# Sending routed rows with a rolling wait of three on four semaphores, in place of groups of four

## The chip, the cores and the metric

The kernel runs on one core of one Trainium2 chip. The metric is the device time of one execution, in microseconds (us); lower is better. The kernel before takes 642.34 us, the median of 3 runs (642.05 to 642.77).

## The reference

Four sequences of 1024 tokens with 256 channels pass through an attention-like block and then a mixture of experts. What matters here is the second part: every token picks two of eight experts, and its normalised row takes part in both.

```python
x = x + _layernorm(_L0_attn_ref(_layernorm(x), Wq, Wk, fc1_w, fc1_b, fc2_w, fc2_b))
x = x + _layernorm(_L0_ffn_ref(_layernorm(x), gate_w, gate_b, w1, b1, w2, b2))

# attention: rotated q and k in bf16, exp(scores) summed over the causal keys,
# one number per token, then 1 -> 16 -> 256 with a relu between
# experts:
logits = flat @ gate_w + gate_b            # 4096 tokens, 8 experts
topv, topi = lax.top_k(logits, 2)
topw = softmax(topv)
for each expert e:
    h = gelu(flat @ w1[e] + b1[e])         # 256 -> 1024
    out = h @ w2[e] + b2[e]                # 1024 -> 256
    final += out * routing[:, e]
```

## The kernel before

The work has two stages that overlap a little.

**First stage, four sequences one after another ("batches" 0 to 3).** TensorE projects, scores and turns; ScalarE takes the exponentials; VectorE measures, normalises, chooses the two experts of each token and computes for each of its two copies a row number in `sorted_x`, a table in HBM where every expert has a region. `place_rows` (VectorE) ends with the semaphore `rows_ready`. GpSimd (POOL) then sends the batch: 16 indirect DMAs (8 tiles of 128 tokens, two copies), each of 128 rows of 260 numbers (`send_rows`, line 185). A row holds the token's 256 normalised channels and 4 numbers (the "tag": token, first expert, two weights). Batches 0 to 2 are sent from `xrows`, batch 3 from `xrow_last`.

**Second stage, tiles of 256 sorted rows.** SyncE (SP) loads a tile `xt` from `sorted_x` (line 527 for tiles 0 and 1, line 1474 from tile 2 on). TensorE turns it (`pX`, line 455), multiplies by `w1` (`pL`, line 1623, 48 matmuls) and by `w2` (`pY`, line 1635, 48 matmuls), each as three products of high and low halves. VectorE splits the hidden values (`h_lo`, line 1652), and GpSimd adds the two halves of the result `y` to their tokens in `sum_y` with two indirect DMAs (line 533), called scatters below. Tiles 0 and 1 belong to the busiest expert and are computed while batch 3 is still in the first stage; from tile 2 on the loops of `over_tiles` run.

**What sets the order around the change.** Every engine executes its own instructions in order. Those of GpSimd are, for batches 0 to 2: wait for `rows_ready`, four sends, wait until the whole group has landed, four sends, and so on; after the last group `rows_left` is raised. For batch 3 the sends stand without such waits between the scatters of tiles 0 and 1: sends 0 to 5, scatters of tile 0, sends 6 and 7, wait for tile 0's scatters, scatters of tile 1, sends 8 to 10, wait for tile 1's scatters (`y_left`), sends 11 to 15. Then comes the block of tiles 2 and on: it waits for the steering table, reads the number of tiles of the expert (line 1413), and for each tile waits for `y_ready`, issues two scatters, waits until they have landed (`y_sent`) and raises `y_left` (line 77).

VectorE needs `y_left` before it computes the weights of the next tile (`weigh_rows`, line 1661); behind that stand in its order the copy of the tag (`save_tag`, line 464), the taking of `y` (line 1671) and the splitting of the next tile's hidden values. SP loads the next `xt` only once the tag has been copied.

SP itself waited for `rows_sent` to reach the count of two whole batches before it loaded tile 0, and for three or four whole batches from tile 2 on (`load_tile`).

Of the kernel before, what the change touches and what calls it, by code (L numbers as in the profile page):

```python
# [21 lines left out]
B, L, D = 4, 1024, 256  # L22
NT = B * L
KC = D // P
TB = L // P
# [9 lines left out]
AHEAD = 2  # L35
# [22 lines left out]
BATCH_SENT = 2 * TB * 16  # L58
SP_ENDS = 4
END_SENT = NE * 16  # L60
SEND_FIRST = (6, 8, 11)
BURST = 4


RSQRT_LINKS = 10
# [8 lines left out]
def hold(eng, sem, value, passed):  # L74

    eng.wait_ge(sem, value)
    eng.sem_inc(passed, 1)
# [39 lines left out]
def build(nc, x_in, wqT, wkT, fc1_w, fc1_b, fc2_wT, fc2_b, low_rows, gate_w, gate_b, w1, b1T, w2, b2,  # L117
# [7 lines left out]
    with ExitStack() as ctx:  # L125
        def sb(name, shape, dt, c=ctx):
            return c.enter_context(nc.sbuf_tensor(name, shape, dt))

        def sem(name, c=ctx):
            return c.enter_context(nc.semaphore(name))  # L130
# [29 lines left out]
        sb("rows_kept", [P, TB, XW], F32)  # L160
        fill = sb("fill", [P, TM // P, XW], F32)
        slot_i = sb("slot_i", [P, 2 * 2 * TB], I32)
        rows_sent = sem("rows_sent")
        tile_in = sem("tile_in")
        b1_taken = sem("b1_taken")
        passed = sem("passed")
# [7 lines left out]
        def load_second(sp, e, par):  # L174
# [2 lines left out]
                         w2[bass.ds(e, 1), :, :].rearrange("e (c p) d -> p (e c) d", p=P)  # L177
                         ).then_inc(weights_in[par][1], 16)

        def send_rows(pool, c, which):  # L180

            rows = xrow_last if c == B - 1 else xrows[:, c * TB:(c + 1) * TB, :]
            for i in which:
                at = c % 2 * 2 * TB + i
                pool.indirect_dma_start(  # L185
                    out=sorted_x, out_offset=bass.IndirectOffsetOnAxis(ap=slot_i[:, at:at + 1], axis=0),
                    in_=rows[:, i % TB, :], in_offset=None).then_inc(rows_sent, 16)

# [217 lines left out]
        rows_left = sem("rows_left")  # L408
# [70 lines left out]
        def _(sp):  # L479
# [39 lines left out]
            e1 = sp.value_load(busy_i[0:1, 2:3].bitcast(I32), min_val=0, max_val=NE - 1)  # L519
            load_first(sp, e1, 1)  # L520
            load_second(sp, e1, 1)
            sp.wait_ge(rows_sent, AHEAD * BATCH_SENT)
            for g in range(AHEAD):
                if g > 0:
                    sp.wait_ge(tile_turned, g)
# [6 lines left out]
        def scatter_rows(pool, i, rows, to, sent=y_sent):  # L532
            pool.indirect_dma_start(  # L533
                out=sum_y, out_offset=bass.IndirectOffsetOnAxis(ap=to[:, i:i + 1], axis=0),
                in_=rows[:, i, :], in_offset=None,
                compute_op=ALU.add).then_inc(sent, 16)

        @block.gpsimd
        def _(pool):
            def scatter_ahead(pool, g):  # L540

                for i in range(TM // P):
                    pool.wait_ge(y_ready, 2 * g + i + 1)
                    scatter_rows(pool, i, ys_ahead[g], dests_ahead[g])

            pool.sem_inc(rows_left, 2)
# [12 lines left out]

            for b in range(B - 1):  # L560
                pool.wait_ge(rows_ready, b + 1)
                for first in range(0, 2 * TB, BURST):
                    if first > 0:
                        hold(pool, rows_sent, b * BATCH_SENT + first * 16, passed)
                    send_rows(pool, b, range(first, first + BURST))
                hold(pool, rows_sent, (b + 1) * BATCH_SENT, rows_left)

            pool.sem_inc(y_left, ONE)
            pool.wait_ge(sums_cleared, 16)
# [6 lines left out]
            send_rows(pool, B - 1, range(SEND_FIRST[1], SEND_FIRST[2]))  # L576
            hold(pool, y_sent, 64, y_left)
            send_rows(pool, B - 1, range(SEND_FIRST[2], 2 * TB))

        @block.scalar  # L580
        def _(act):
# [882 lines left out]
        def _(sp):  # L1464
# [4 lines left out]

            def load_tile(sp, word):  # L1470

                hold(sp, rows_sent, (word & 1) * BATCH_SENT + (B - 1) * BATCH_SENT, passed)
                hold(sp, ends_filled, (word & 1) * END_SENT + ONE, passed)
                sp.dma_start(xt[:], sorted_x[bass.ds(word >> 1, TM), :].rearrange("(a p) c -> p a c", p=P)
                             ).then_inc(tile_in, 16)
# [17 lines left out]
            word = tile_word(sp, 0)  # L1493
# [4 lines left out]
            word = tile_word(sp, 1)  # L1498
# [3 lines left out]
            word = sp.value_load(steer[0:1, C_TILES + NP - 1:C_TILES + NP], min_val=0, max_val=WORD_MAX)  # L1502
# [339 lines left out]
```

## Time and profile before

| | before |
|---|---|
| median of 3 runs | 642.34 us |
| the profiled execution | 638.7 us |
| its span | 636.9 us |
| mean granted TensorE clock | 0.936 |
| TensorE matmul busy | 545.6 us, 86% |
| VectorE busy | 424.5 us, 67% |
| ScalarE busy | 365.3 us, 57% |
| GpSimd busy | 187.3 us, 29% |

The span is the profiled execution from its first to its last instruction; 1.8 us of its time lie outside. A busy share is an average over both stages. From about 234 us on the path is mostly TensorE's, save where the experts change; before that it shares the path with VectorE and others. For each send or scatter the profile shows GpSimd's time to write the descriptors, about 1 us for a send and 1.6 us for a scatter; the data moves after that, on queue q0 (SP's transfers move on q1).

### The profile page before, as it was taken

Reading aid. Unit: us, or ns where it says so; the run is one execution under the profiler, and the core shown is the slowest. Engines: PE = TensorE matmul, PEld = TensorE weight load, DVE = VectorE, ACT = ScalarE, POOL = GpSimd, SP = SyncE. Lnnn points to the kernel's source line nnn. Section 1 sums busy time; section 2 is a strip of 40 time slices with the busy share of each in tenths; the row PEclk is TensorE's granted clock in tenths of the full one; section 3 lists DMA queues with packets and bytes.
Section 4 is the critical chain, followed back from the end, with each engine's and each line's share of the span. In section 5 each row is a group of like instructions: output and inputs, shape, how many; then the busy total and the mean of one; then the engine's idle time right before and its main releaser. Section 6 shows DMA issues by size and latency. Waiting matters only on the chain.

```text
span 636.9 us, 14628 instructions
## 1 busy us (share of the span) xinstructions
PE 545.6 (86%) x4170; PEld 500.3 (79%) x4175; DVE 424.5 (67%) x1444; ACT 365.3 (57%) x836; POOL 187.3 (29%) x153
## 2 busy tenths in 40 slices
PE   1968788686896989999999999999999999999940
PEld 1737365462775989999999989989998999998940
DVE  5799698996887665545555557487388655455477
ACT  3455766684570746364554665685688563553582
POOL 2000045244535653242322412312312232421320
PEclk9968969798797999999999999999999999999985
DMA  8930011362215833232232353384374232322479
GB/s 216 361 118 1 1 67 67 114 236 87 90 43 185 237 87 60 50 44 39 52 48 50 45 161 63 58 247 91 46 246 88 51 50 50 44 39 50 99 186 326
DMA packets 51853, 66.79 MB, mean 105 GB/s; under 512 B 4870, under 2 KB 45292, under 8 KB 51692
## 3 DMA queue, kind: packets, MB, share of 16 engines
q1 hardware_dynamic: 37804, 47.87, 23.9%
q0 software_dynamic: 14016, 18.56, 16.9%
q8 instruction: 11, 0.18, 0.1%
q14 instruction: 22, 0.18, 0.1%
HBM read 38.26 MB, written 28.74 MB: 105 GB/s over the span
## 4 chain that ended last, share of the span: by engine, by line
PE 68%; DVE 16%; issue 5%; ACT 4%; DMA 4%; POOL 1%; DVEq 1%; SPq 0%; POOLq 0%; ACTq 0%
PE pY L1635 28%; PE pL L1623 24%; PE pP L759 6%; DMA sum_y<-y,dest 3%; PE pP L861 2%; PE pS L776 2%; PE pX L455 2%; DVE z L1775 2%; DVE mstats L1003 2%; PE pT L744 1%; ACT probs L657 1%; PE pS L818 1%; ACT xrows L631 1%; POOL sum_y L533 1%; DMA x_all<-x 1%
## 5 line engine op out<-in xcount | busy, mean ns | idle before, releaser
L1558 ACT ACTIVATE h<-pL,b_now 128x256 f32<-128x256 f32 x272 | 112.3, 463 | 151.7 <-PE pL L1623 146.7
L533 POOL DMA_INDIRECT sum_y<-y,dest x68 | 110.2, 1621 | 269.4 <-DVE y L1679 256.9
L1635 PE MATMUL pY<-w_hi,h_lo 128*128 128x256 f32 x544 | 154.0, 283 | 3.5 <-DVE h_lo L1652 3.4
L1623 PE MATMUL pL<-xeT_hi,w_lo 128*128 128x256 f32 x544 | 151.4, 278 | 6.2 <-issue 6.1
L1652 DVE TENSOR_TENSOR h_lo<-h,h_hi 128x512 fp32r<-128x512 f32 x136 | 92.7, 691 | 91.7 <-ACT h_hi L1564 90.9
L1635 PE MATMUL pY<-w_hi,h_hi 128*128 128x256 f32 x544 | 150.7, 277 | 0.6 <-issue 0.6
L1623 PE MATMUL pL<-xeT_lo,w_hi 128*128 128x256 f32 x544 | 150.7, 277 | 0.0
L1635 PE MATMUL pY<-w_lo,h_hi 128*128 128x256 f32 x544 | 150.6, 277 | 0.0
L1623 PE MATMUL pL<-xeT_hi,w_hi 128*128 128x256 f32 x544 | 150.6, 277 | 0.0
L1623 PEld LDWEIGHTS pL<-xeT_hi,w_lo 128*128 128x128 f32 x544 | 102.0, 188 | 7.6 <-issue 7.6
L1635 PEld LDWEIGHTS pY<-w_hi,h_lo 128*128 128x128 f32 x544 | 102.2, 188 | 5.1 <-DVE h_lo L1652 4.6
L1635 PEld LDWEIGHTS pY<-w_lo,h_hi 128*128 128x128 f32 x544 | 102.4, 188 | 0.8 <-issue 0.8
L1635 PEld LDWEIGHTS pY<-w_hi,h_hi 128*128 128x128 f32 x544 | 102.3, 188 | 0.0
L1623 PEld LDWEIGHTS pL<-xeT_lo,w_hi 128*128 128x128 f32 x544 | 102.1, 188 | 0.0
L1623 PEld LDWEIGHTS pL<-xeT_hi,w_hi 128*128 128x128 f32 x544 | 102.1, 188 | 0.0
L1564 ACT ACTIVATE h_hi<-h 128x512 fp32r<-128x512 f32 x136 | 86.0, 632 | 6.3
L185 POOL DMA_INDIRECT sorted_x<-xrows,slot_i x48 | 49.2, 1026 | 128.5 <-DVE xrows L1144 89.6
L1671 DVE SCALAR_TENSOR_TENSOR y<-pY,b_all 128x256 f32<-128x256 f32 x66 | 27.8, 421 | 44.5 <-PE pY L1635 44.5
L200 DVE TENSOR_TENSOR w_lo<-w_stage,w_hi 128x512 fp32r<-128x512 f32 x64 | 42.4, 688 | 14.4 <-ACT w_hi L193 9.1
L193 ACT ACTIVATE w_hi<-w_stage 128x512 fp32r<-128x512 f32 x64 | 36.8, 620 | 0.0
L744 PE MATMUL pT<-ident,xn 128*128 128x128 f32 x64 | 17.6, 430 | 19.2 <-ACT xn L588 11.3
L608 ACT ACTIVATE qk<-pP 128x512 bf16<-128x512 f32 x32 | 19.0, 592 | 21.5 <-PE pP L759 20.4
(292 smaller groups left out, 847.5 us busy)
## 6 DMA issues: line engine op xcount, KB each, us to landing
w_stage<-w SPq DMA_DIRECT2D x16, 1024.0 KB
xt<-sorted_x SPq DMA_DIRECT2D x38, 260.0 KB
sum_y<-fill SPq DMA_DIRECT2D x1, 4352.0 KB, 19.9
w_stage<-sum_y SPq DMA_DIRECT2D x8, 512.0 KB, 8.0
out<-z SPq DMA_DIRECT2D x8, 512.0 KB, 5.9
x_all<-x SPq DMA_DIRECT2D x3, 1024.0 KB, 8.3
sorted_x<-fill SPq DMA_DIRECT2D x8, 260.0 KB
sum_y<-y,dest POOLq DMA_INDIRECT x68, 3.7
```

Of the source, the lines that this page charges most:

```text
L185: pool.indirect_dma_start(out=sorted_x, out_offset=bass.IndirectOffsetOnAxis(ap=slot_i[:, at:at + 1], axis=0), in_=rows[:, i % TB, :], in_ ...
L193: act.activation(w_hi[par][:, i, q * WQ:(q + 1) * WQ], w_stage[par][:, i, q * WQ:(q + 1) * WQ], ACT.Copy).then_inc(w_hi_ready[i], 1)
L200: low = dve.tensor_tensor(w_lo[par][:, i, piece], w_stage[par][:, i, piece], w_hi[par][:, i, piece].bitcast(F32), ALU.subtract)
L533: pool.indirect_dma_start(out=sum_y, out_offset=bass.IndirectOffsetOnAxis(ap=to[:, i:i + 1], axis=0), in_=rows[:, i, :], in_offset=None, c ...
L744: mm = pe.transpose(pT[:, n % 2, u * P:(u + 1) * P], xn[:, t, k * P:(k + 1) * P], ident[:])
L759: mm = pe.matmul(pP[:, n % 2, :], w[:, k, i, mo], x[:, k, tok], start=(k == 0 and w is wqk_lo), stop=(k == KC - 1 and x is xT_lo))
L1558: a = act.activation(h[:, c, :], pL[:, bk, i * TM:(i + 1) * TM], ACT.Gelu, bias=b1_now[par][:, c:c + 1])
L1564: act.activation(h_hi[:, 2 * bk:2 * bk + 2, :], h[:, 2 * bk:2 * bk + 2, :], ACT.Copy).then_inc(h_hi_ready, 1)
L1623: mm = pe.matmul(pL[:, bk, i * TM:(i + 1) * TM], w[:, 0, col], x[:, k, :], start=(k == 0 and w is lo), stop=(k == KC - 1 and x is xeT_lo))
L1635: mm = pe.matmul(pY[:, i, 0:D], s[:, c, rows], w[:, 1, c * D:(c + 1) * D], start=(c == 0 and s is h_lo), stop=(c == FC - 1 and w is lo))
L1652: dve.tensor_tensor(h_lo[:, cs, :], h[:, cs, :], h_hi[:, cs, :].bitcast(F32), ALU.subtract).then_inc(h_split, 1)
L1671: dve.scalar_tensor_tensor(out=y[:, i, :], in0=pY[:, i, 0:D], scalar=1.0, in1=b2_all[:, bass.ds(who, 1), :].rearrange("p e d -> p (e d)"), ...
```

## The change

The sends go to four semaphores in turn, `rows_sent0` to `rows_sent3`. Send i of a batch, for i of 3 and more, first waits until send i-3 has landed. After the 16th the last three are waited for, and `rows_left` is raised; this is new for batch 3. The scatters of tiles 0 and 1 have such a wait too. SP waits for `rows_left` where it waited for `rows_sent`.

```diff
-BURST = 4
+LANES = 4
+LAG = 3
...
-        rows_sent = sem("rows_sent")
+        rows_sent = [sem(f"rows_sent{lane}") for lane in range(LANES)]
...
+        def landed(pool, c, i):
+
+            pool.wait_ge(rows_sent[i % LANES], c * BATCH_SENT // LANES + (i // LANES + 1) * 16)
+
         def send_rows(pool, c, which):
 
             rows = xrow_last if c == B - 1 else xrows[:, c * TB:(c + 1) * TB, :]
             for i in which:
                 at = c % 2 * 2 * TB + i
+                if i >= LAG:
+                    landed(pool, c, i - LAG)
                 pool.indirect_dma_start(
                     out=sorted_x, out_offset=bass.IndirectOffsetOnAxis(ap=slot_i[:, at:at + 1], axis=0),
-                    in_=rows[:, i % TB, :], in_offset=None).then_inc(rows_sent, 16)
+                    in_=rows[:, i % TB, :], in_offset=None).then_inc(rows_sent[i % LANES], 16)
...
-            sp.wait_ge(rows_sent, AHEAD * BATCH_SENT)
+            sp.wait_ge(rows_left, 2 + AHEAD)
...
                     pool.wait_ge(y_ready, 2 * g + i + 1)
+                    landed(pool, B - 1, SEND_FIRST[g] - LAG + i)
                     scatter_rows(pool, i, ys_ahead[g], dests_ahead[g])
...
                 pool.wait_ge(rows_ready, b + 1)
-                for first in range(0, 2 * TB, BURST):
-                    if first > 0:
-                        hold(pool, rows_sent, b * BATCH_SENT + first * 16, passed)
-                    send_rows(pool, b, range(first, first + BURST))
-                hold(pool, rows_sent, (b + 1) * BATCH_SENT, rows_left)
+                send_rows(pool, b, range(2 * TB))
+                for i in range(2 * TB - LAG, 2 * TB):
+                    landed(pool, b, i)
+                pool.sem_inc(rows_left, 1)
...
             send_rows(pool, B - 1, range(SEND_FIRST[2], 2 * TB))
+            for i in range(2 * TB - LAG, 2 * TB):
+                landed(pool, B - 1, i)
+            pool.sem_inc(rows_left, 1)
...
-                hold(sp, rows_sent, (word & 1) * BATCH_SENT + (B - 1) * BATCH_SENT, passed)
+                hold(sp, rows_left, (word & 1) + 2 + B - 1, passed)
```

GpSimd's instructions from a batch of the middle, before. One row is one instruction or several alike; in brackets stand the semaphores that it waits for.

```order
L185 DMA sorted_x<-xrows,slot_i 34816x260 [waits rows_sent,rows_ready]
L185 DMA sorted_x<-xrows,slot_i 34816x260 x3
L185 DMA sorted_x<-xrows,slot_i 34816x260 [waits rows_sent]
L185 DMA sorted_x<-xrows,slot_i 34816x260 x3
L185 DMA sorted_x<-xrows,slot_i 34816x260 [waits rows_sent]
```

The same place in the changed kernel, its first seven sends:

```order
L192 DMA sorted_x<-xrows,slot_i 34816x260 [waits rows_sent3,rows_sent1,rows_sent2,rows_ready]
L192 DMA sorted_x<-xrows,slot_i 34816x260 x2
L192 DMA sorted_x<-xrows,slot_i 34816x260 [waits rows_sent0]
L192 DMA sorted_x<-xrows,slot_i 34816x260 [waits rows_sent1]
L192 DMA sorted_x<-xrows,slot_i 34816x260 [waits rows_sent2]
L192 DMA sorted_x<-xrows,slot_i 34816x260 [waits rows_sent3]
```

No send has moved. One wait in four sends has become one at each from the fourth on.

GpSimd from the wait for tile 1's scatters to the first scatter of tile 2, before:

```order
L185 DMA sorted_x<-xrow_last,slot_i 34816x260 [waits y_sent]
L185 DMA sorted_x<-xrow_last,slot_i 34816x260 x4
L1527 UNCONDITIONAL_BRANCH
L1451 UNCONDITIONAL_BRANCH [waits steer_ready]
L1451 ISA
L1413 TENSOR_LOAD steer
L1413 ISA x2
L1438 REGISTER_ALU
L1438 COMPARE_AND_BRANCH
L76 REGISTER_ALU x2
L76 ISA
L533 DMA sum_y<-y,dest 4352x256 [waits y_ready]
```

The same place in the changed kernel:

```order
L192 DMA sorted_x<-xrow_last,slot_i 34816x260 [waits y_sent,rows_sent0]
L192 DMA sorted_x<-xrow_last,slot_i 34816x260 [waits rows_sent1]
L192 DMA sorted_x<-xrow_last,slot_i 34816x260 [waits rows_sent2]
L192 DMA sorted_x<-xrow_last,slot_i 34816x260 [waits rows_sent3]
L192 DMA sorted_x<-xrow_last,slot_i 34816x260 [waits rows_sent0]
L1537 UNCONDITIONAL_BRANCH [waits rows_sent3,rows_sent1,rows_sent2]
L1461 UNCONDITIONAL_BRANCH [waits steer_ready]
L1461 ISA
L1423 TENSOR_LOAD steer
L1423 ISA x2
L1448 REGISTER_ALU
L1448 COMPARE_AND_BRANCH
```

The branch that leaves the first stage now waits for the last three sends; all that follows on GpSimd stands behind it.

## Rows read from the trace of the kernel before

**Rows 1.** The page's busy time: engine, us (share of the span) x instructions.

```profile
PE 545.6 (86%) x4170; PEld 500.3 (79%) x4175; DVE 424.5 (67%) x1444; ACT 365.3 (57%) x836; POOL 187.3 (29%) x153
```

**Rows 2.** The chain that ended last, 240 to 637: start us, us, what.

```profile
251.75 0.44 PE pX L455 x4
252.19 5.46 PE pY L1635 x48
```

**Rows 3.** The chain again, 196 to 245.

```profile
213.07 8.30 DMA sum_y<-y,dest
...
221.39 0.03 POOLq L77
...
224.25 2.23 DMA xt<-sorted_x
...
234.97 5.44 PE pL L1623 x48
240.41 0.44 PE pX L455 x4
```

**Rows 4.** Timeline of GpSimd, 78 to 125: start, us, instruction [idle before, releaser].

```profile
82.27 1.06 POOL L185 DMA_INDIRECT sorted_x<-xrows,slot_i  x1 [76.68 <-DVE xrows L1144]
...
86.22 0.97 POOL L185 DMA_INDIRECT sorted_x<-xrows,slot_i  x1 [0.30 <-issue]
89.48 0.96 POOL L185 DMA_INDIRECT sorted_x<-xrows,slot_i  x1 [2.29 <-DMA sorted_x<-xrows,slot_i]
```

**Rows 5.** Line 77, whole span: count, ns min/median/max, first and last start.

```profile
L77 POOLq EVENT_SEMAPHORE  x114: 17/17/17, 88.7 to 614.1; - x114
```

**Rows 6.** Timeline of GpSimd, 125 to 245: inside batch 1, and the start of batch 3.

```profile
130.34 0.96 POOL L185 DMA_INDIRECT sorted_x<-xrows,slot_i  x1 [6.49 <-DMA sorted_x<-xrows,slot_i]
...
193.98 0.97 POOL L185 DMA_INDIRECT sorted_x<-xrow_last,slot_i  x1 [10.66 <-DVE xrow_last L1144]
```

**Rows 7.** Timeline of SP, 100 to 275: loads of tiles 0 and 1.

```profile
153.48 4.42 SPq L527 DMA_DIRECT2D xt<-sorted_x  x2
```

**Rows 8.** Timeline of VectorE, 146 to 176: the tag of tile 0.

```profile
156.26 0.20 DVE L464 COPY tag<-xt 128x8 f32<-128x8 f32 x1
```

**Rows 9.** Timeline of TensorE, 150 to 170.

```profile
156.24 1.11 PE L804 MATMUL pT<-ident,xt 128*128 128x128 f32 x4 [3.86 <-DMA xt<-sorted_x]
158.61 1.12 PE L787 MATMUL pT<-ident,hid 128*128 128x128 f32 x4 [1.26 <-DVE hid L994]
```

**Rows 10.** Window 160 to 166: length, engines' busy us, then PEclk, DMA share, GB/s.

```profile
160.00:166.00 6.00, 5.58 (x28) 5.36 (x29) 4.47 (x23) 3.30 (x7) 3.04 (x4) 0.50 0.23 83
```

**Rows 11.** Timeline of GpSimd, 125 to 245, from batch 3's send 11 on.

```profile
222.17 0.96 POOL L185 DMA_INDIRECT sorted_x<-xrow_last,slot_i  x1 [3.23 <-DMA sum_y<-y,dest]
...
227.50 1.50 POOL L185 DMA_INDIRECT sorted_x<-xrow_last,slot_i  x1 [0.30 <-issue]
229.30 1.61 POOL L533 DMA_INDIRECT sum_y<-y,dest  x1 [0.30 <-issue]
231.21 1.91 POOL L533 DMA_INDIRECT sum_y<-y,dest  x1 [0.30 <-issue]
```

**Rows 12.** GpSimd's queue in 229 to 230, then 230 to 231: packets, MB, share.

```profile
q0 software_dynamic: 40, 0.12, 33.3%
...
q0 software_dynamic: 8, 0.01, 4.3%
```

**Rows 13.** GpSimd's sequencer: line 1451 in 222 to 226, line 77 in 224 to 227.

```profile
L1451 POOLq FUSED_REGOPS  x1: 86/86/86, 223.9 to 223.9; - x1
...
L77 POOLq EVENT_SEMAPHORE  x2: 17/17/17, 225.2 to 225.9; - x2
```

**Rows 14.** Timeline of VectorE, 184 to 275: weights and tag behind y_left of tile 2.

```profile
235.48 0.17 DVE L1661 CAST dest<-tag 128x2 int32<-128x2 f32 x1 [1.60 <-POOLq L77]
...
236.23 0.17 DVE L464 COPY tag<-xt 128x8 f32<-128x8 f32 x1
```

**Rows 15.** SP's queue in 239 to 239.5, tile 5's load: packets, MB, share.

```profile
q1 hardware_dynamic: 119, 0.11, 62.8%
```

## The prediction

> **What bounds the kernel now.** I read the busy time first: TensorE 86%, GpSimd 29% [rows 1]. So GpSimd's own work is no bound, and a change of its waits counts only where somebody waits for what it sends. Then the chain that ended last. From 234.97 on it is TensorE alone: 5.4 us for `pL`, 0.44 for the turn, 5.46 for `pY`, tile after tile, with no idle time between them [rows 2, 3]. A delay of TensorE there is not won back, since it has no slack to win it from, and loads of weights follow its progress. Between 213 and 227 the chain goes through GpSimd: a scatter of tile 1 takes until 221.4 to land, raises `y_left`, VectorE copies the tag, SP loads a tile, TensorE turns it [rows 3]. The question is then which of the kernel's waits on sends lies on the chain, and I went through them in the timelines of GpSimd, SP, VectorE and TensorE.
>
> **Part one: batches 0 to 2, where groups of four become a rolling wait.** In the first group the fourth send starts at 86.22, the semaphore is passed at 88.7, and the next send starts at 89.48 [rows 4, 5]. So a send lands 2.5 us after its start, and a blocked instruction starts 0.8 us after its release. Sends that don't wait follow each other every 1.3 us ((86.22 - 82.27) / 3). With the new rule send i waits for a landing at start(i-3) + 2.5, may start at + 3.3, and would start at + 3.9 anyway: free by 0.6 us. Four sends then take 5.3 us instead of 89.48 - 82.27 = 7.2 [rows 4], and a batch of 16, with its three gaps, starts its last send about 6 us earlier.
>
> Who gains from it? In batch 1 the gaps are larger, the first 6.49 us [rows 6], since 4 MB of weights are loaded beside it; I estimate that it lands 4 to 6 us earlier. SP waited for it and issued tile 0's load at 153.48 [rows 7]; this load will move to about 148. But VectorE copied the tag at 156.26 without any idle time before it [rows 8], in the middle of its own work: it came no later for the load. TensorE did wait for it, 3.86 us, and turned the tile at 156.24; but its next work, the turn of `hid` at 158.61, waited for VectorE [rows 9]. With the tile there early TensorE turns it at about 152.5 and waits longer after it. After batch 2 GpSimd sits idle for 10.66 us until VectorE has batch 3 ready [rows 6], and batch 0 ends before batch 1 begins. **Part one: 0 us.** The bounds: nothing lost, and at best 0.7 us gained, if an early turn kept TensorE's clock up. It was at half level, 1.2 GHz, in 160 to 166 [rows 10], and the turn at 158.61 took 1.12 us for four matmuls where the four of a `pX` take 0.44 [rows 2, 9]; the first layer's matmuls that follow lie beside 9 us of VectorE's work. I take 0: its idle time gets longer, not shorter.
>
> **Part two: batch 3, where waits are new.** Its sends had none. By the same 2.5 + 0.8 < 3.9 most of the new ones are met before they are reached. In front of each scatter of tiles 0 and 1 the send waited for was issued at least 4 us earlier. Sends 11 to 15 start at 222.17 to 227.50 [rows 11] and wait for 8 to 12; the first is held until 221.39 by tile 1's scatters in any case. For 14 and 15 I find 0.1 to 0.3 us each. Taken: 0.1 for the last one. From below 0; from above, if every wait cost as long as the group's gap of 2.29 [rows 4] for the five, 11 us. I take the low end because the waits are for a send three ahead and not for the last one.
>
> **Part three: the wait behind the last send.** This is the step that costs. Before, GpSimd's sequencer did not wait for the sends: it reached the loop of tile 2 at 223.9 and its first semaphore there at 225.2 [rows 13], while three sends had not even started, and both scatters stood queued when send 15 ended. They started at 229.30 and 231.21 [rows 11]. Now the branch out of the first stage waits for the landing of sends 13, 14 and 15.
>
> - Landing of send 15: started at 227.50, it moved most of its data in 229 to 230 and the rest in 230 to 231 [rows 11, 12]. 227.50 + 2.5 = 230.0 is the earliest, 231.0 the latest; with the 0.1 above I take 230.6.
> - From there to the loop 0.2 us (two branches; an estimate, since the trace shows the sequencer there only behind dispatches), through the loop's head 225.2 - 223.9 = 1.3 [rows 13], to the start of the scatter 0.8 [rows 4, 5]: 230.6 + 2.3 = 232.9, against 229.30. Later by 3.6 us.
> - The pair took 3.8 us from the first start to the last end, one of the two a slow 1.91 [rows 11]. At 1.6 each and 0.3 between them it is 3.5, so 3.3 of the 3.6 are left. Landing after that took 235.44 - 233.12 = 2.3 [rows 11, 14] and stays.
>
> `y_left` of tile 2 comes at 238.7 instead of 235.4. VectorE was already waiting for it, 1.60 us [rows 14], so all of the 3.3 goes on: to the tag at 236.23, to taking `y` of tile 3, to the splits of tile 4, and through the tag to SP's load of tile 5. That load's last data moved just before 239.5 [rows 15], and TensorE turned the tile at 240.41 right after `pL` [rows 3]. From the last data to the turn some 0.4 us pass, so it was ready for TensorE at about 240.0: slack 0.4 us, from 0.2 to 0.6. TensorE is idle for 3.3 - 0.4 = **2.9 us** before that turn. The splits of tile 4 on VectorE shift with it and don't add to it. One tile later the slack is larger: its `y_left` moves by about 3 us and TensorE by 2.9, so nothing is lost twice, and nothing is given back.
>
> Bounds of part three: from below 2.1 us (release at 230.0, slack 0.6, the pair at its shortest), from above 3.8 (release at 231.0, slack 0.2, the pair as slow as before).
>
> On the first bullet the Trainium skill says something of its own ("Advanced Engine Details and Errata", Sequencer Loop and Engine Queue Depths): while an engine instruction waits in its queue, the sequencer goes on reading; GpSimd's queue holds 8. The trace agrees with it: at 223.9 the sequencer was past sends that start at 224.7 to 227.5 [rows 11, 13]. By that rule a wait on a send itself, which stays in the queue, leaves the run ahead as it was, and only the wait on the branch ends it. Were the branch's wait also left in the queue, part three would cost 0.
>
> **Part four: SP.** `rows_left` in place of `rows_sent` costs no more instructions. For tile 2's load it is raised long before; a tile that needs all four batches is loaded later than 231 in both kernels. 0 us.
>
> **Sum.** 0 + 0 + 2.9 + 0 = 2.9, on the profiled execution's 638.7 (span 636.9 and 1.8 around it): 641.6. The profiled execution is 3.6 us faster than the median of the runs, 642.34; I add the term to the median: **645.2 us**.
>
> **The rivals.**
>
> *The end of batch 3 is hidden after all: no change.* The wait is met earlier than I think, or in the timed runs, which are 3.6 us longer than the profiled one, `y_left` of tile 2 has more slack. Against it: VectorE stood waiting [rows 14], and TensorE's slack is under 1 us. Time: 642.3 + 0 to 1.2, so 642.3 to 643.5.
>
> *Faster: tile 0's load was on the path in the timed runs.* In the profile its slack is nearly nothing: TensorE turned the tile at 156.24, VectorE copied the tag at 156.26 [rows 8, 9]. If in the other executions weights and sends crowd each other more, the load lands 1 to 3 us later, VectorE waits, and behind it `hid`, the whole attention end and the routing of batch 3. The rolling wait takes that out. It decides where the load of tile 0 lands more than 2.9 us after VectorE wants it, or where it is late at all and part three is hidden. Time: 642.3 - 1 to - 3, so 639.5 to 641. For it speaks the 3.6 us between profile and runs; against it that nothing says where they lie.
>
> *More than forecast: batch 3's rolling waits hold each other.* Tile 1's scatter takes 8.3 us to land [rows 3], beside a load of the next expert's weights. If sends 8 to 10 land as slowly, each of 12 to 15 starts later, and with them the last landing. One slow link of 1 to 3 us is added in full: 646.2 to 648.2. For it speaks batch 1's gap of 6.49; against it that in 229 to 231 only 0.13 MB are left to move [rows 12].
>
> *The change doesn't do what it says.* The order of instructions shows the waits where the text puts them. No chance of its own.
>
> **How the numbers follow.** Forecast 0.52, with its own range of 643.9 to 646.3 (parts two and three from 1.6 to 4.0); hidden 0.19; faster 0.15; more 0.14. A difference within 0.2%, 1.3 us, can't be told from none here. Faster than 641.06: 0.15. Slower than 643.62: the forecast and the rival above it, 0.66, less 0.01 for its lowest edge: 0.65. Within: 0.20. The range leaves out some 0.1 at either end: 641.2 to 647.4.
>
> **What would show it.** GpSimd's timeline: sends of batches 0 to 2 every 1.3 us, with an idle time of some 17 us before batch 3 in place of 10.66; sends of batch 3 as before to 0.3 us; then an idle time of 3 to 4 us before the first scatter of tile 2, which starts at about 233. VectorE's wait for `y_left` of tile 2: 4.5 to 5 us instead of 1.60. TensorE idle for 2.5 to 3.3 us before the turn of tile 5, with the load as releaser. SP's load of tile 0 at about 148, and `hid` still turned at 158.6. I am wrong if the scatter starts before 231, if TensorE's idle time there is under 1.5 us, or if VectorE's work around 155 to 160 has moved.

## The result: 668.17 us, and where the profile after shows it

The changed kernel takes 668.17 us (median of 4 runs, 667.02 to 669.96), the kernel before 642.19 us (641.74 to 642.77): ratio 1.0425, 95% interval 1.0397 to 1.0453. It is slower by 26 us, where 2.9 us were forecast. The profiled execution took 669.96 us (span 668.2). It is 1.8 us longer than its median and that of before 3.5 us shorter than its own, so the two traces differ by 31.3 us, more than the kernels do: 21.4 by the start of batch 3, 27.0 by the turn of tile 5 (267.40 against 240.41), and 4.3 behind it that nothing here explains.

The page of after, busy time and clock; the rows of before are in [rows 1].

```profile
PE 553.9 (83%) x4174; PEld 506.7 (76%) x4175; DVE 424.2 (63%) x1444; ACT 366.0 (55%) x836; POOL 186.2 (28%) x153
```

TensorE does the same work (553.9 us), over a longer span. The loss is idle time. Where it begins is seen in the timelines. GpSimd's in batch 0 (columns: start, duration, instruction, idle time before it), against [rows 4]:

```profile
83.05 1.06 POOL L192 DMA_INDIRECT sorted_x<-xrows,slot_i  x1 [77.46 <-DVE xrows L1154]
...
102.33 0.97 POOL L192 DMA_INDIRECT sorted_x<-xrows,slot_i  x1 [0.30 <-issue]
```

The sends follow each other every 1.28 us without a pause, to the last of batch 0, as forecast. Batch 1 was to start at 119; it starts at 130.79. ScalarE's timeline of the same stretch says why:

```profile
95.80 0.60 ACT L618 ACTIVATE qk<-pP 128x512 bf16<-128x512 f32 x1 [0.72 <-issue]
...
97.19 0.19 ACT L633 ACTIVATION_READ_ACCUMULATOR probs<-x_all,minus_mean 128x1 f32 x1
105.64 1.08 ACT L618 ACTIVATE qk<-pP 128x512 bf16<-128x512 f32 x2 [8.26 <-remote]
```

Its work ends at 97.4, and then it stands for 8.26 us in front of the next `qk`. In program order this `qk` waits for TensorE alone: for the sixth matmul of a projection. That one started at 95.84, and the profile has it done at 96.2, before ScalarE stood at all. The projection after it was issued too, up to 97.78:

```profile
95.84 0.39 PE L769 MATMUL pP<-xT_lo,wqk_hi 128*128 128x512 f32 x1
...
97.78 0.40 PE L769 MATMUL pP<-xT_lo,wqk_hi 128*128 128x512 f32 x1
106.38 0.77 PE L769 MATMUL pP<-xT_hi,wqk_lo 128*128 128x512 f32 x1 [8.21 <-ACT qk L618]
```

and TensorE stood itself for 8.21 us until ScalarE went on. The page puts ScalarE's wait down to "remote", that is to no engine whose work ended at that time: what it waits for is TensorE's increment of a semaphore, and TensorE's work was done. (The profile models the ends of matmuls; they are rough.) I call such an idle time of ScalarE a stop. The same happens twice in batch 2, at `h` (8.53 and 4.94 us), while the sends of that batch run:

```profile
173.03 0.19 ACT L216 ACTIVATE b_now<-b_all 128x8 f32 x1
178.16 0.84 ACT L689 ACTIVATE h<-pP,b_now 128x256 f32<-128x256 f32 x2 [4.94 <-remote]
...
188.05 0.84 ACT L689 ACTIVATE h<-pP,b_now 128x256 f32<-128x256 f32 x2 [8.53 <-remote]
```

Not all of the 4.94 us is lateness: the twelfth matmul that this `h` needs started at 175.32 and was done at 175.7, so the increment came 2.4 us late. The 8.53 us are all of that kind, since the matmuls were done at 178.3.

```profile
175.32 0.41 PE L828 MATMUL pP<-xeT_lo,w_hi 128*128 128x256 f32 x1
```

ScalarE's waits in 80 to 262 (line, waited for: us in total, times, longest), the two without a known releaser and, for comparison, `qk`'s ordinary one:

```profile
ACT h L689 <- remote: 13.6, 3, 8.5
...
ACT qk L618 <- remote: 8.3, 1, 8.3
ACT qk L618 <- PE pP L769: 7.3, 5, 2.6
```

Three such stops of 8.3, 4.9 and 8.5 us move batch 1 by 11.7 us and batch 3 by 21.4: its first send starts at 215.42 and not at 193.98. The rest is batch 3. There the waits are met where the forecast puts them, but they last longer:

```profile
215.42 0.97 POOL L192 DMA_INDIRECT sorted_x<-xrow_last,slot_i  x1 [27.60 <-DVE xrow_last L1154]
...
237.30 1.02 POOL L192 DMA_INDIRECT sorted_x<-xrow_last,slot_i  x1 [0.31 <-issue]
...
245.74 0.96 POOL L192 DMA_INDIRECT sorted_x<-xrow_last,slot_i  x1 [4.88 <-DMA sorted_x<-xrow_last,slot_i]
...
251.34 1.22 POOL L192 DMA_INDIRECT sorted_x<-xrow_last,slot_i  x1 [0.59 <-DMA sorted_x<-xrow_last,slot_i]
257.35 1.60 POOL L540 DMA_INDIRECT sum_y<-y,dest  x1 [4.80 <-issue]
```

Send 11 (245.74) waits 4.88 us for the landing of send 8. It starts 245.74 - 215.42 = 30.3 us after the batch's first send; before it was 222.17 - 193.98 = 28.2 [rows 6, 11]. The scatter of tile 2 follows an idle time of 4.80 us (forecast 3 to 4), 257.35 - 215.42 = 41.9 us after the first send; before it was 229.30 - 193.98 = 35.3. VectorE's wait for `y_left` of tile 2 is 9.65 us and not 1.60 [rows 14], and TensorE stands 4.09 us before the turn of tile 5 (forecast 2.5 to 3.3):

```profile
263.18 0.17 DVE L1671 CAST dest<-tag 128x2 int32<-128x2 f32 x1 [9.65 <-POOLq L78]
```

```profile
267.40 1.11 PE L462 MATMUL pX<-ident,xt 128*128 128x128 f32 x4 [4.09 <-DMA xt<-sorted_x]
```

### The profile page after: what moved, and what is told of

The parts are those of the page before. It is cut to its first block, busy times and chain, and to the rows that moved or that the text cites. A ratio compares the mean times of both kernels' runs of the same rounds, so it can differ in the third digit from the quotient of the medians.

```text
span 668.2 us, 14632 instructions
## 1 busy us (share of the span) xinstructions
PE 553.9 (83%) x4174; PEld 506.7 (76%) x4175; DVE 424.2 (63%) x1444; ACT 366.0 (55%) x836; POOL 186.2 (28%) x153
## 4 chain that ended last, share of the span: by engine, by line
PE 59%; DVE 14%; DMA 8%; issue 7%; ACT 4%; another core or an unknown queue 3%; POOL 2%; DVEq 1%; POOLq 1%; SPq 0%; ACTq 0%
PE pY L1645 24%; PE pL L1633 21%; PE pP L769 5%; DMA sum_y<-y,dest 4%; DMA sorted_x<-xrow_last,slot_i 2%; PE pP L871 2%; DVE z L1785 2%; PE pX L462 2%; PE pS L786 1%; DVE mstats L1013 1%; PE pT L754 1%; POOL sum_y L540 1%; POOL sorted_x L192 1%; PE pS L828 1%
## 5 line engine op out<-in xcount | busy, mean ns | idle before, releaser
L1681 DVE SCALAR_TENSOR_TENSOR y<-pY,b_all 128x256 f32<-128x256 f32 x66 | 27.7, 420 | 46.0 <-PE pY L1645 46.0
L207 DVE TENSOR_TENSOR w_lo<-w_stage,w_hi 128x512 fp32r<-128x512 f32 x64 | 42.3, 686 | 14.5 <-ACT w_hi L200 9.1
L618 ACT ACTIVATE qk<-pP 128x512 bf16<-128x512 f32 x32 | 18.9, 594 | 33.1 <-PE pP L769 20.3
L769 PE MATMUL pP<-xT_hi,wqk_lo 128*128 128x512 f32 x64 | 29.5, 461 | 8.5 <-ACT qk L618 8.2
```

The source lines that it names most:

```text
L207: low = dve.tensor_tensor(w_lo[par][:, i, piece], w_stage[par][:, i, piece], w_hi[par][:, i, piece].bitcast(F32), ALU.subtract)
L618: act.activation(qk[:, i, m, h * 512:(h + 1) * 512], pP[:, n % 2, :], ACT.Copy).then_inc(qk_ready, 1)
L769: mm = pe.matmul(pP[:, n % 2, :], w[:, k, i, mo], x[:, k, tok], start=(k == 0 and w is wqk_lo), stop=(k == KC - 1 and x is xT_lo))
L1681: dve.scalar_tensor_tensor(out=y[:, i, :], in0=pY[:, i, 0:D], scalar=1.0, in1=b2_all[:, bass.ds(who, 1), :].rearrange("p e d -> p (e d)"), ...
```

## The experiments

Eighteen runs follow, on four chips, each measured beside the kernel before on the same chip. The chips turned out to be of two kinds, which decide most of what follows, so the table of ratios comes first. On chips 1 and 2 the kernel before takes 636.7 us; on chips 10 and 15 it takes 640.3 to 641.8, as on the chip of the result above (642.2), whose number is not known. With so few chips, "kind" is a name for what was seen, and what makes the kinds is open. "Rolling" is the wait for the send three ahead.

| kernel | batches 0 to 2 | in batch 3 | behind last send | chips 1, 2 | chips 10, 15 |
|---|---|---|---|---|---|
| e3 | groups of 4 | no | yes | 1.0040 | |
| e1, g1, h1 | one row of 16 | no | no | 0.9997, 0.9988 | **1.0498** |
| i1 | groups of 8 | no | no | | 1.0030 |
| i2 | 4, then small memsets | no | no | | 1.0122 |
| i3 | rolling, two ahead | no | no | | 1.0024 |
| f3 | rolling | no | no | | **1.0329** |
| e4, g2 | rolling | no | yes | 1.0062, 1.0051 | |
| f4 | rolling | yes | no | | **1.0322** |
| after (g4, f1) | rolling | yes | yes | 1.0130 | **1.0376** (the result: **1.0425**) |
| e2, g3, h2 | groups of 4 | yes | yes | 1.0146, 1.0105 | 1.0081 |
| h3 | groups of 4 | pause before send 14 | no | | 1.0014 |

### Chip 1: the row of sends, the last wait, the waits of batch 3

e1_group16, the kernel before with a longer group:

```diff
-BURST = 4
+BURST = 16
```

> The kernel before with the sends of batches 0 to 2 in one group of sixteen on its one semaphore: no pause inside a batch, no new semaphore, no new wait, batch 3 untouched. If it is the unbroken row of sends that holds ScalarE up (the changed kernel's trace has ScalarE idle for 8.3 us in batch 0 and for 4.9 and 8.5 us in batch 2, with TensorE long done), the same idle times come back here and the time is 655 to 664 us. If the four semaphores or the waiting sends do it, or if the loss arises in batch 3, the time is 642 us and ScalarE goes through batches 0 to 2 as in the kernel before.

Measured: 637.64 us against 636.75, ratio 0.9997 (0.9971 to 1.0024). No stop of ScalarE. By my expectation this speaks against the row of sends. That reading was wrong, since the changed kernel had not been run on this chip.

e2_groups_back, the changed kernel with groups in batches 0 to 2:

```diff
-                send_rows(pool, b, range(2 * TB))
-                for i in range(2 * TB - LAG, 2 * TB):
-                    landed(pool, b, i)
+                for first in range(0, 2 * TB, LANES):
+                    send_rows(pool, b, range(first, first + LANES), rolling=False)
+                    for i in range(first, first + LANES):
+                        landed(pool, b, i)
```

> The changed kernel with groups of four back in batches 0 to 2, still on four semaphores; batch 3 keeps its waiting sends and the wait behind the last one. If the unbroken row of sends is the cause, batch 3 starts at 194 us as before and only the terms of the prediction for batch 3 are left: 645 to 648 us. If the four semaphores are the cause, or the waits of batch 3, the time stays at 662 to 668 us.

Measured: 646.96 us, ratio 1.0146 (1.0116 to 1.0177): 10.2 us. In us this is inside the expected 645 to 648, but that range was laid on a kernel before of 642.2, and here it takes 636.75: as a ratio it lies above the 1.004 to 1.009 meant, and below the 1.03 to 1.04 of the other case. Batch 3 starts at 194.48.

e3_last_wait, the kernel before with one wait more:

```diff
             send_rows(pool, B - 1, range(SEND_FIRST[2], 2 * TB))
+            hold(pool, rows_sent, B * BATCH_SENT, passed)
```

> The kernel before with one wait more, behind the last send of batch 3, on its one semaphore. This is the term that the prediction priced at 2.9 us (2.1 to 3.8) alone: 645.1 us (644.3 to 646.0), the first scatter of tile 2 at about 233 us instead of 229.3. If the wait costs more than its landing, because the landing is slow behind a full row of sends, 647 us or more; if it is hidden, 642 us.

Measured: 639.25 us, ratio 1.0040 (1.0005 to 1.0075): 2.5 us, with an interval of 0.3 to 4.8. The term of part three, priced at 2.9 (2.1 to 3.8), by itself. The median hides something: the ten runs fall in two bunches, six at 637.2 to 639.6 and four at 644.5 to 647.6, where the 21 runs of the kernel before lie in 634.9 to 640.4. The trace is of the upper bunch (644.52) and goes through batch 3 and on to 400 like e4's (638.40); in 400 to 500 TensorE is busy for 93.23 us where e4's is for 95.86. What the upper bunch is, no run shows.

e4_rolling_012, the changed kernel with no waits inside batch 3:

```diff
-                if i >= LAG:
+                if c < B - 1 and i >= LAG:
...
-                    landed(pool, B - 1, SEND_FIRST[g] - LAG + i)
```

> The changed kernel without its waits inside batch 3 (sends and scatters there run as in the kernel before); the waiting sends of batches 0 to 2 and the wait behind the last send stay. If the loss arises in batches 0 to 2, with 2.9 us for the last wait, the time is 664 to 668 us and the idle times of ScalarE in batches 0 and 2 stay. If the waits of batch 3 carry it, 645 us.

Measured: 640.54 us, ratio 1.0062 (1.0031 to 1.0093), without any stop of ScalarE though the sends of batches 0 and 2 run in rows of sixteen. The diff leaves out one thing: without waits inside batch 3, the wait behind the last send covers the last four sends and not three. No single part carried 26 us, which left the chip as a suspect.

### Chip 10: the changed kernel again, and its parts

f1_after_again is the changed kernel, f2_before_again the kernel before for its trace. f3_rolling_012_alone has neither the waits inside batch 3 nor the one behind its last send, f4_inner_only lacks the last one alone; in both SyncE waits itself:

```diff
-                hold(sp, rows_left, (word & 1) + 2 + B - 1, passed)
+                for lane in range(LANES):
+                    hold(sp, rows_sent[lane], ((word & 1) + B - 1) * (BATCH_SENT // LANES), passed)
```

> The changed kernel once more, on the chip of the day, beside its own kernel before. If the idle times of ScalarE (8.3, 4.9 and 8.5 us in batches 0 and 2) belong to the change, the ratio is 1.042 again. The four runs so far say that neither unbroken sends nor the inner waits of batch 3 alone bring them, so the rival is that they came with one launch or one chip: then they are absent here and the ratio is 1.010 to 1.018.

> The kernel before, for its trace on the same chip as the others: ScalarE's idle time of 4.8 us that ends at 229.5 us in the first trace of it, and the scatter of tile 2. If such idle times come with the launch, this one can be gone, and the scatter of tile 2 starts at about 224.6 us as in the kernel with groups of sixteen.

> The changed kernel without the waits inside batch 3 and without the wait behind its last send; SyncE waits for the four semaphores itself before it loads a tile. Only the waiting sends of batches 0 to 2 are left. By the prediction they cost nothing: ratio 1.000 (0.998 to 1.002), since the kernel with the last wait alone stood at 1.0040 and that with both at 1.0062. If they cost by themselves, 1.003 or more.

> The changed kernel with the waits inside batch 3, but without the wait behind its last send (SyncE waits for the four semaphores itself). If the waits inside batch 3 are what costs, 5 to 8 us are left: ratio 1.008 to 1.013. If they cost only together with the last wait, under 2 us: 1.003 or less.

Measured: the changed kernel 666.02 us against 641.73, ratio 1.0376 (1.0327 to 1.0425), with the stops; f3 662.02, 1.0329 (1.0273 to 1.0386); f4 662.00, 1.0322 (1.0269 to 1.0374). So here the waiting sends of batches 0 to 2, priced at 0, cost 20.3 us alone. The waits inside batch 3 add nothing by themselves, and the last wait on top of them 4.0. The traces of f3 and f4 offer a reason for the 0: without the new waits tile 1's scatters hold send 11 just as long, 29.65 us after the batch's first send (242.90 - 213.25), and with them it starts at 29.70 (243.49 - 213.79):

```profile
242.90 0.96 POOL L192 DMA_INDIRECT sorted_x<-xrow_last,slot_i  x1 [3.56 <-DMA sum_y<-y,dest]
```

```profile
243.49 0.96 POOL L192 DMA_INDIRECT sorted_x<-xrow_last,slot_i  x1 [4.02 <-DMA sorted_x<-xrow_last,slot_i]
```

The trace of before (637.77 us, one run) has two short stops in batch 3 (2.6 and 2.1 us). f3's ScalarE in batches 0 to 2:

```profile
ACT qk L614 <- remote: 9.5, 2, 4.8
ACT h L685 <- remote: 8.7, 2, 7.1
```

### Chip 2: is it the chip?

g1 is e1, g2 is e4, g3 is e2, and g4_after_third the changed kernel, each unchanged.

> The kernel before with groups of sixteen, once more: the first time it stood at 1.000 on a chip where no kernel showed TensorE's and ScalarE's common idle times, while the changed kernel had three of them (21 us) on another chip. If the unbroken row of sends brings them on some chips and not on others, this kernel shows them wherever the changed kernel of this same call does: ratio 1.025 to 1.035 there, and 1.000 where it does not. If the four semaphores or the waits inside the row bring them, this kernel has none and stays at 1.000 while the changed kernel has them.

> The changed kernel without its waits inside batch 3, once more (1.006 the first time, no such idle times, while its neighbour without the last wait stood at 1.033 on another chip). If it is the chip that decides: 1.033 to 1.038 where the changed kernel of this call stands at 1.04. If it is the placing of GpSimd's instructions: 1.006 again whatever the changed kernel does.

> The changed kernel with groups of four back in batches 0 to 2, once more (1.0146 the first time). If the pauses between the groups keep the idle times away on every chip: 1.008 to 1.015 here too, and batch 3 starts at 193 to 195 us even where it starts at 215 us in the changed kernel of this call. If not the pauses but the chip did it: 1.03 or more where the changed kernel stands at 1.04.

> The changed kernel a third time, as the reference for the three kernels above on the chip of this call: 1.038 to 1.043 with the idle times of batches 0 and 2 if the chip is like the first and the third, 1.010 to 1.018 without them if it is like the second.

Measured: 0.9988 (0.9958 to 1.0018), 1.0051 (1.0019 to 1.0083), 1.0105 (1.0048 to 1.0163), and the changed kernel 645.41 us against 636.69, **1.0130** (1.0093 to 1.0168). The same program that loses 24 to 26 us elsewhere loses 8.7 here. Two traces of the same program in 8.2 us from some 14.5 us after the first send of batch 0, and in 6 us behind it, first that of the result, then g4's (columns: busy us and instructions of each engine, granted clock, DMA share, GB/s):

```profile
97.40:105.60 8.20, 0.77 (x4) 0.29 (x2) 3.37 (x15) 0.00 (x0) 4.67 (x5) 0.85 0.27 97
106.00:112.00 6.00, 5.62 (x17) 4.50 (x18) 3.97 (x6) 2.26 (x5) 0.00 (x0) 0.67 0.00 0
```

```profile
96.40:104.60 8.20, 6.32 (x40) 4.86 (x38) 7.92 (x17) 6.42 (x15) 4.24 (x5) 1.00 0.23 81
105.00:111.00 6.00, 6.00 (x30) 2.09 (x29) 3.91 (x25) 3.50 (x9) 0.00 (x0) 1.00 0.00 0
```

The sends are the same (5 on GpSimd, 97 and 81 GB/s). ScalarE does 6.42 us of work on this chip, and none on the other. Behind the stop TensorE's granted clock is 0.67 in place of 1.00, a stretch partly at the lower of its two levels (1.2 and 2.4 GHz); before it, it had stood for 8.21 us. That part of the loss outlasts the stop.

What the waits inside batch 3 cost here is the difference of g4 and g2, 645.41 - 639.82 = 5.6 us. On chip 1 the same difference is that of e2 and e3, 646.96 - 639.25 = 7.7. Both hang on the lower bunch of the kernels without these waits: g2 too has three of ten runs at 643.5 to 646.2, like e3, and g4 and e2 have none of theirs below 642.5. g4's timeline shows a place, and SyncE's what lies beside it:

```profile
212.87 1.08 POOL L192 DMA_INDIRECT sorted_x<-xrow_last,slot_i  x1 [0.30 <-issue]
...
215.55 0.96 POOL L192 DMA_INDIRECT sorted_x<-xrow_last,slot_i  x1 [0.30 <-issue]
220.18 1.21 POOL L192 DMA_INDIRECT sorted_x<-xrow_last,slot_i  x1 [3.68 <-DMA sorted_x<-xrow_last,slot_i]
...
230.90 1.60 POOL L540 DMA_INDIRECT sum_y<-y,dest  x1 [4.13 <-issue]
```

```profile
212.51 0.41 SPq L171 DMA_DIRECT2D w_stage<-w  x1
213.10 0.37 SPq L177 DMA_DIRECT2D w_stage<-w  x1
```

SyncE issues both halves of the next expert's weights at 212.51 and 213.10. In 214 to 217 SyncE's queue (q1) has 84% of the 16 DMA engines' time and GpSimd's (q0) 7%:

```profile
q1 hardware_dynamic: 215, 0.88, 84.0%
q0 software_dynamic: 42, 0.03, 6.9%
```

Send 8 (212.87) lands so late that send 11 stands 3.68 us, and 12 to 15 with it: it starts 27.6 us after the batch's first send (e2 28.6, g3 28.0). Without the waits inside batch 3 it can start earlier. In e4's trace it follows at 24.2 without a wait (e1, g1 and e3: 24.1); in g2's, a run of 646.23 us, tile 1's scatters hold it to 27.7, as in g4. First e4's, then g2's:

```profile
217.72 0.96 POOL L192 DMA_INDIRECT sorted_x<-xrow_last,slot_i  x1 [0.30 <-issue]
```

```profile
220.57 0.96 POOL L192 DMA_INDIRECT sorted_x<-xrow_last,slot_i  x1 [3.18 <-DMA sum_y<-y,dest]
```

So some 3.5 us of the 5.6 are seen, where the scatters would have let send 11 go. The last wait comes on top: in g4 the scatter follows an idle time of 4.13.

### Chip 15: unbroken rows against semaphores

h1 is e1 and h2 is e2, unchanged. h3_pause_batch3 is the kernel before with a pause in its last row of sends:

```diff
-            send_rows(pool, B - 1, range(SEND_FIRST[2], 2 * TB))
+            send_rows(pool, B - 1, range(SEND_FIRST[2], SEND_FIRST[2] + 3))
+            hold(pool, rows_sent, (B - 1) * BATCH_SENT + (SEND_FIRST[2] + 3) * 16, passed)
+            send_rows(pool, B - 1, range(SEND_FIRST[2] + 3, 2 * TB))
```

> The kernel before with groups of sixteen a third time. It stood at 1.000 on two chips on which the kernel before takes 636.7 us and the changed kernel 1.013. On a chip on which the kernel before takes about 642 us, and the changed kernel 1.04: 1.025 to 1.035 with idle times of ScalarE in batches 0 and 2, if the unbroken row of sends is what brings them; 1.000 if the semaphores or the waits of the row bring them. On a chip of the first kind it is 1.000 again and tells nothing new.

> The changed kernel with groups of four back in batches 0 to 2, a third time (1.010 and 1.015 on chips on which the kernel before takes 636.7 us). On a chip with 642 us for the kernel before: 1.008 to 1.016 if the pauses between groups are what keeps TensorE's increments moving, 1.03 or more if the four semaphores are the cause.

> The kernel before with a pause in batch 3's last row of sends: GpSimd waits for all that it has sent before the last two. If an unbroken row holds TensorE's increments up there too (4.8 us of ScalarE's idle time that ends at 229.5 us in the first trace), this kernel is 1 to 4 us faster than before on a chip with 642 us for the kernel before, and 0 to 1.5 us slower on one with 636.7 us, since the scatter of tile 2 starts some 2.5 us later.

Measured: h1, with one semaphore and no wait in the row, 673.93 us against 641.81, **1.0498** (1.0470 to 1.0526), more than I expected; h2, with four semaphores and all waits but in groups, 646.11, 1.0081 (1.0049 to 1.0112). That settles it: on such a chip the unbroken row is enough, and the four semaphores and the waits in and behind batch 3 are not. ScalarE's waits in h1, then in e1, the same program on chip 1:

```profile
ACT qk L608 <- remote: 20.8, 4, 7.7
...
ACT h L679 <- remote: 9.3, 1, 9.3
```

```profile
ACT qk L608 <- PE pP L759: 9.3, 9, 2.0
...
ACT h L679 <- PE pP L818: 3.8, 2, 2.6
```

In h1 batch 1 is unbroken too, and has stops of 4.85 and 6.92 us; this is most likely why it loses more than the changed kernel. There the rolling wait finds landings late, beside the loads of weights, and makes gaps of 4.72 and 2.58 us by itself, and in that batch the changed kernel has no stop:

```profile
134.62 0.97 POOL L192 DMA_INDIRECT sorted_x<-xrows,slot_i  x1 [0.30 <-issue]
140.31 0.97 POOL L192 DMA_INDIRECT sorted_x<-xrows,slot_i  x1 [4.72 <-DMA sorted_x<-xrows,slot_i]
...
146.41 0.97 POOL L192 DMA_INDIRECT sorted_x<-xrows,slot_i  x1 [2.58 <-DMA sorted_x<-xrows,slot_i]
```

h3: 642.87 us, 1.0014 (0.9990 to 1.0038). The stop in batch 3, 4.8 us in the first trace of before, is down to 0.2 us in this one, but send 14 now follows an idle time of 2.65 us. No gain.

### Chip 10 once more: how long a row, and what a pause must be

i1_group8 has `BURST = 8`; i3_lag2 is f3 with `LAG = 2`; i2_work_between, from the kernel before:

```diff
-                        hold(pool, rows_sent, b * BATCH_SENT + first * 16, passed)
+                        for k in range(5):
+                            pool.memset(spare[:], 0.0).then_inc(spare_set, 1)
+                            pool.wait_ge(spare_set, 5 * (b * 3 + first // BURST - 1) + k + 1)
```

> The kernel before with groups of eight in batches 0 to 2: half as many pauses. On a chip with 642 us for the kernel before, where groups of four stand at 1.000 and sixteen at 1.050: 1.01 to 1.035 if the holding up grows with the length of the row, 1.000 if a row of eight (10 us) is still short enough. On a chip with 636.7 us for the kernel before: 1.000 whatever is the case.

> The kernel before with five small memsets on GpSimd (of a tile that nothing reads, each behind the last) in place of the wait for landing between two groups of four. GpSimd doesn't stand still for a landing and has no semaphore of a DMA to wait for, but it issues no send for about a microsecond. If the absence of sends is what lets TensorE's increments through: no idle times of 4 to 9 us, ratio 0.998 to 1.003. If it takes the wait itself, so that what was sent has landed: 1.02 to 1.05 on a chip with 642 us for the kernel before, and 1.000 on one with 636.7 us.

> The changed kernel with each send of batches 0 to 2 waiting for the one two ahead, and no waits in and behind batch 3. A send lands some 2.5 us after its start and the wait sees it 0.8 us later, so there is a pause of 0.7 to 0.9 us behind each send and no row is unbroken. On a chip with 642 us for the kernel before: 1.000 to 1.004, if a short pause behind each send is enough (with three ahead it was 1.033); 1.02 or more if it takes the longer pause behind a group. On one with 636.7 us: 0.999 to 1.003.

Measured against 640.25 us: i1 641.79, 1.0030 (1.0003 to 1.0057); i3 642.33, 1.0024 (0.9997 to 1.0052); i2 647.93, 1.0122 (1.0060 to 1.0184). Rows of eight bring one long stop in the three batches, 4.94 us (2.4 of it behind the end of the matmuls that it waits for). It ends at 166.44, 1.5 us behind the end of the eighth send of batch 2, in the pause:

```profile
164.01 0.97 POOL L185 DMA_INDIRECT sorted_x<-xrows,slot_i  x1 [0.31 <-issue]
167.25 0.97 POOL L185 DMA_INDIRECT sorted_x<-xrows,slot_i  x1 [2.27 <-DMA sorted_x<-xrows,slot_i]
```

```profile
161.31 0.19 ACT L209 ACTIVATE b_now<-b_all 128x8 f32 x1
166.44 0.84 ACT L679 ACTIVATE h<-pP,b_now 128x256 f32<-128x256 f32 x2 [4.94 <-remote]
```

With two ahead in place of three GpSimd is idle for 0.30 to 0.72 us before a send of batch 0, where an unbroken row has 0.30 before each. So at most 0.4 us were added at a send, mostly at every second, and 2.1 us over the row. That is less than the 0.7 to 0.9 behind each that I expected. There is no stop in batches 0 to 2:

```profile
85.47 0.96 POOL L192 DMA_INDIRECT sorted_x<-xrows,slot_i  x1 [0.54 <-DMA sorted_x<-xrows,slot_i]
86.78 0.96 POOL L192 DMA_INDIRECT sorted_x<-xrows,slot_i  x1 [0.34 <-DMA sorted_x<-xrows,slot_i]
...
91.15 0.96 POOL L192 DMA_INDIRECT sorted_x<-xrows,slot_i  x1 [0.72 <-DMA sorted_x<-xrows,slot_i]
```

i2 has none of over 1.3 us either. Its groups stand 1.05 us apart in place of 0.30 (0.77 us of memsets and the idle time around them), without a wait for a landing, so time without sends is enough. i1, i2 and i3 also speak against a rival, that the sends only meet ScalarE's work at a bad moment: in 95 to 104, where after and h1 have their stops of batch 0, all three send too, and have none. i2's 7.7 us lie elsewhere: batch 3 starts at 194.94, but from 250 on its TensorE does 4% fewer matmuls in the same time, at full clock and without idle time:

```profile
250.00:380.00 130.00, 128.56 (x1132) 128.36 (x1131) 68.39 (x204) 70.94 (x154) 37.65 (x23) 1.00 0.32 56
```

```profile
250.00:380.00 130.00, 128.56 (x1087) 128.36 (x1087) 65.36 (x198) 67.39 (x145) 36.64 (x23) 1.00 0.28 45
```

(the first row is i1's, the second i2's). i2 holds one tile more, of 32 bytes per partition, ahead of others. Whether the placing does it was not tried, so i2's total says nothing on the rows.

## Why the prediction was wrong, step by step

**Part one, batches 0 to 2: 0 us, measured 20.3 on the kind of chip that the result comes from** (f3, 662.02 - 641.73; interval 17 to 25), and 0 to 1.3 on the other (e1 and g1 at 1.000 and 0.999; e4 less e3, 640.54 - 639.25, within the intervals of both). This is the step that failed: the claim that a change of pauses counts only where somebody waits for the sends. Its bookkeeping was right: sends every 1.3 us, the batch done earlier, nobody who gains. On a chip without stops it holds to the end: in e4 tile 0 is loaded at 149.45 (forecast 148) and its tag copied at 155.9 (before 156.3). What cost was not a wait for the sends, but TensorE's increments, which reached ScalarE late while they ran. I asked who waits for the sends and found nobody; I did not ask what the pauses between them were good for. The bounds (-0.7 to 0) came from this question alone. The trace of before held a hint that I passed by. Its one row of five sends [rows 11] ends at 229.0, and there ScalarE has just stood for 4.84 us without a releaser:

```profile
223.98 0.63 ACT L1564 ACTIVATE h_hi<-h 128x512 fp32r<-128x512 f32 x1
229.45 0.84 ACT L1558 ACTIVATE h<-pL,b_now 128x256 f32<-128x256 f32 x2 [4.84 <-remote]
```

Such a stop of 4.6 to 6.5 us near the end of batch 3 stands also in h1, h2, i1, i2 and i3, and as two shorter ones in f2 and f3: there a row of five sends is enough. h3 removed it and gained nothing.

**Part two, waits inside batch 3: 0.1 us, measured 0 (f4 against f3, chip 10), 5.6 (g4 against g2) and 7.7 (e2 against e3).** The forecast took the landings at 2.5 us; send 8 took some 6.5 in g4 (220.18 - 212.87, less the 0.8 from release to start), beside the loads of weights. The rival with a slow link ("sends 8 to 10 land as slowly") names this, and its 1 to 3 us were too small for chips 1 and 2. On chip 10 tile 1's scatters hold send 11 as long by themselves (29.65 and 29.70 us).

**Part three, the wait behind the last send: 2.9 us (2.1 to 3.8), measured 2.5** alone (e3, interval 0.3 to 4.8, in two bunches) and 4.0 on top of the waits inside (f1 against f4). The mechanism is there in every trace: the scatter waits for the landing. The landing was forecast too short: from the start of send 15 to that of the scatter 5.4 us, and it is 6.0 in the result's trace and 6.7 in e3's. Of the size only the median of e3 can be called right.

**Part four: 0 us.** No run parts it from the rest.

Parts two and three together were 2.9; h2, which has just these beside pauses in batches 0 to 2, lost 4.3 us on chip 15. The signs that I had named: sends at 1.3 us, yes; 17 us idle before batch 3, no, 27.6; the scatter after 3 to 4 us of idle time, 4.80; TensorE idle 2.5 to 3.3 before tile 5, 4.09; tile 0's load at 148, no, at 161; "wrong if VectorE's work around 155 to 160 has moved", and it has, by 11 us. On chip 10 the parts are 20.3, 0 and 4.0, together f1's loss of 24.3. They were taken one on top of the other, so that they add up proves nothing; that the first is five times the last carries the account. The 1.7 us to the 26.0 of the result are within the intervals of both.

## What to carry to other kernels

A pause on one engine can be worth something to others who never wait for it. Before closing gaps, look in the trace for stops without a releaser beside stretches that have no gaps already. A rolling wait one step shorter keeps small gaps for nearly nothing (1.0024 against 1.0329, i3 and f3). And measure on more than one chip before a cause is ruled out: e1 said 1.000 and 1.050 of the same program.

## What the runs showed of the hardware

- While GpSimd issues indirect sends every 1.28 us without a pause, ScalarE can get TensorE's increment late, on chips 10, 15 and that of the result. There the stops are 8.26, 4.94 and 8.53 us, and the matmuls waited for had been done 9.4, 2.4 and 9.8 us before; in h1 20.8 us in four, and 9.3. The traces of chips 1 and 2 have none. Only waits of ScalarE for TensorE were hit for long. In batches 0 to 2 rows of 4 brought no stop of over 1.3 us, rows of 8 one in six, rows of 16 at least one in each batch of h1. Enough against it were up to 0.4 us more at every second send or so (i3), or 0.75 us more behind every fourth (i2).
- A send of 128 rows took some 6.5 us to land beside two loads of weights (g4, send 8), and 2.5 us in the first group of before [rows 4, 5].
- The Trainium skill, "SBUF — State Buffer" (SBUF: two separate sides), says that the engines' ports and the DMA's can't contend, and that TensorE and ScalarE wait for nobody there. By that rule alone the sends would cost ScalarE nothing, 0 in place of 20.3 us. The trace does not agree in its outcome, 0.00 us of ScalarE's work in 8.2; but the rule is on data in SBUF, and the runs do not show that the stop lies there.
- Open: whether the increment or the end of TensorE's last matmul is late (ends are modelled in the trace), what is shared, and why the chips differ.
